# A graph layer with routed experts: five fields per edge record, node tiles spread over the sort, and a new order of loads, stores and statistics

## The reference

```python
xn = layernorm(x)
# 1: edges. segment_sum over src of edge_weight * xn[dst], beside xn itself
h   = concat([xn, segment_sum(edge_weight[:, None] * xn[dst], src, N)], axis=1)
gnn = relu(h @ gnn_W + gnn_b)
# 2: mixing of each node's channels: scaled projection to 768 channels, batch norm over the nodes,
#    relu, a grouped product, linear attention within groups of 32, projection back to 256
mix = expmap0(residual_projection(attention(batchnorm(project(logmap0(xn))))))
x   = x + gnn + mix
# 3: two of eight experts for each node
xt      = layernorm(x)
logits  = xt @ Wr + br                       # [3125, 8]
w, e    = top 2 of softmax(logits), w normalised to 1
y_e     = gelu((xt * ln_g[e] + ln_b[e]) @ W1[e] + b1[e]) @ W2[e] + b2[e]   # W1: 256 x 1024
out     = x + sum over both experts of w * y_e
```

## Time and profile before

| | |
|---|---|
| timed runs | 1204.49, 1205.29, 1206.28 us |
| profiled execution | 1207.6 us, span of its instructions 1205.8 us |
| TensorE (PE), busy | 990.7 us, 82% of the span |
| VectorE (DVE) | 770.8 us, 64% |
| POOL (GpSimd) | 636.9 us, 53% |
| ScalarE (ACT) | 590.9 us, 49% |
| mean granted TensorE clock | 0.899 of 2.4 GHz |
| DMA | 106.10 MB, mean 88 GB/s |

### The profile page before, as it was taken

How to read it: one execution, slowest core, us unless ns; L and a number is a source line. 1 busy time by engine, 2 the same in 40 slices (tenths; PEclk the granted TensorE clock), 3 DMA queues, 4 the chain that set the end, 5 groups by cost and what they waited for, 6 DMA issues and landing times.

```text
span 1205.8 us, 20167 instructions
## 1 busy us (share of the span) xinstructions
PE 990.7 (82%) x5432; PEld 800.6 (66%) x5433; DVE 770.8 (64%) x1705; ACT 590.9 (49%) x1528; POOL 636.9 (53%) x610
## 2 busy tenths in 40 slices
PE   2789859996687677777777767299999999999995
PEld 1356535553466566666565436299999999999995
DVE  9999956664577777777777788634444444444441
ACT  0455425556867776666765653133333333333331
POOL 4392247777777777776766750214443333333332
PEclk9799969997888888888888877599999999999998
DMA  7012123333333333333333449732222222222221
GB/s 171 24 41 89 33 58 103 104 105 104 102 101 101 104 101 102 105 97 92 97 97 96 133 161 377 264 93 37 35 38 39 39 35 35 35 39 36 40 36 18
DMA packets 55071, 106.10 MB, mean 88 GB/s; under 512 B 15337, under 2 KB 37070, under 8 KB 52822
## 3 DMA queue, kind: packets, MB, share of 16 engines
q0 software_dynamic: 31312, 70.38, 23.4%
q1 hardware_dynamic: 23075, 33.97, 8.8%
q10 hardware_dynamic: 611, 0.92, 0.3%
HBM read 86.55 MB, written 18.69 MB: 87 GB/s over the span
## 4 chain that ended last, share of the span: by engine, by line
PE 51%; DVE 26%; issue 12%; DMA 3%; DVEq 3%; ACT 2%; POOL 2%; ACTq 0%; POOLq 0%
PE ps L759 17%; PE ps L769 16%; PE ps L630 7%; DVE arena_c L1226 6%; PE ps L677 5%; DVE arena_a L1157 4%; PE ps L639 4%; DVE arena_a L1151 2%; DMA arena_c<-y_d,arena_e 2%; POOL arena_c L513 2%; DVEq L1214 1%; PE ps L749 1%; DVE arena_c L1276 1%; ACT arena_e L860 1%; DVEq L1212 1%
## 5 line engine op out<-in xcount | busy, mean ns | idle before, releaser
L513 POOL DMA_INDIRECT arena_c<-y_d,arena_e x415 | 407.8, 983 | 147.6 <-issue 87.7
L630 PE MATMUL ps<-arena_c,arena_e 128*125 128x256 f32 x830 | 255.3, 431 | 113.7 <-DVE arena_c L1226 87.0
L630 PEld LDWEIGHTS ps<-arena_c,arena_e 128*125 128x125 f32 x830 | 161.0, 212 | 191.5 <-issue 155.4
L1226 DVE TENSOR_TENSOR arena_c<-arena_c,ps 125x256 f32 x415 | 172.5, 416 | 100.3 <-PE ps L630 85.5
L539 POOL DMA_INDIRECT out<-node,bn x56 | 101.0, 1804 | 250.1 <-DVE node L1506 247.1
L860 ACT ACTIVATE arena_e<-arena_e 128x125 f32<-128x125 bf16 x415 | 190.6, 509 | 70.1 <-PE ps L630 57.0
L984 ACT ACTIVATE arena_d<-ps,small 128x128 f32<-128x128 f32 x448 | 121.6, 383 | 186.5 <-PE ps L759 151.5
L769 PE MATMUL ps<-arena_c,arena_d 128*128 x896 | 202.5, 379 | 0.0
L769 PEld LDWEIGHTS ps<-arena_c,arena_d 128*128 128x128 f32 x896 | 166.0, 190 | 20.3
L759 PEld LDWEIGHTS ps<-node,arena_d 128*128 128x128 f32 x896 | 107.2, 196 | 2.6 <-DVE node L1498 1.2
L759 PE MATMUL ps<-node,arena_d 128*128 128x128 f32 x896 | 107.4, 279 | 0.8 <-DVE node L1498 0.8
(11 more groups left out here) (318 smaller groups left out, 1370.3 us busy)
## 6 DMA issues: line engine op xcount, KB each, us to landing
arena_c<-in_W SPq DMA_DIRECT2D x8, 1024.0 KB, 9.3
arena_a<-in_W SPq DMA_DIRECT2D x8, 1024.0 KB, 12.7
arena_c<-y_d,arena_e POOLq DMA_INDIRECT x415, 2.8
x<-in_x SPq DMA_DIRECT2D x5, 560.0 KB
z_d<-x SPq DMA_DIRECT2D x5, 560.0 KB
out<-x SPq DMA_DIRECT2D x5, 560.0 KB
y_d<-arena_c SPq DMA_DIRECT2D x15, 125.0 KB
y_d<-arena_a SPq DMA_DIRECT2D x10, 125.0 KB
```

What stands on the lines that cost most here:

```text
L513: pool.indirect_dma_start(ring[:, b % GR, :], None, io["y_d"], bass.IndirectOffsetOnAxis(gix[:, b:b + 1], 0)).then_inc(gth[b % GR], 16)
L630: nc.tensor.matmul(pair(b), sel[b % SR], ring[:, b % GR, :], start=True, stop=True).then_inc(g_mm, 1)
L1226: V.tensor_tensor(part, part, pair(b), ALU.add).then_inc(g_acc, 1)
```

## The change

- An edge record has five fields. `dst` is stored as one 16-bit number, 0x3000 + dst, whose bits are read as bfloat16 through the placing matmul, and read back as an integer with one VectorE operation. One of the two bit operations, two casts and the buffer behind them go.
- `tiles_to(k)` spreads the 15 node tiles over chunks 1 to 18 instead of 0 to 14.
- SP loads `x` only when `src` has landed. POOL makes the two masks first, then splits the weights (as soon as they have landed), and only then the other index rows and the zero fill. ScalarE waits for that fill before its sixth turned copy instead of before its first tile.
- Every third sum `max(ACC, 0) + X` (tiles 2, 5, ..., 23) is made by POOL in two operations; SP, TensorE and VectorE wait for its semaphore `n_p` at those tiles.
- The logits' matmul has 48 columns instead of 96. ScalarE's two roots stand after tile 23 and after tile 24. VectorE computes `rz` and `zbias` behind the choice of experts.
- SP waits for the first two fetched blocks, then loads W2 of experts 5 and 6, then `b2s`, then stores `out`.

```diff
-NF = 6
+NF = 5
+CODE = 0x3000
-WIDE = 12
+WIDE = 6
+def tiles_to(k):
+    return AHEAD + min((NT - AHEAD) * k // (NK - 1), NT - AHEAD)
+def third(t):
+    return (t + 1) // 3
...
         def _(sp):
+            sp.wait_ge(ld_src, 16)
             x_t = io["x"].rearrange("(t p) c -> p t c", p=T)
...
-            sp.wait_ge(zeroed, 1 + 2 * (SPARE // BQ // EG))
+            sp.wait_ge(zeroed, 1 + SPARE // BQ // EG)
...
-                sp.wait_ge(n_x, t + 5)
+                sp.wait_ge(n_x, t + 5 - third(t + 4))
+                sp.wait_ge(n_p, third(t + 4))
...
-            sp.dma_start(b2s, io["b2"].partition_broadcast(128)).then_inc(b_in, 16)
+            sp.wait_ge(xs_in[0], 16)
+            sp.wait_ge(xs_in[1], 16)
             for e in (5, 6):
                 load_w2(e)
+            sp.dma_start(b2s, io["b2"].partition_broadcast(128)).then_inc(b_in, 16)
...
# POOL
-            P.memset(zero, 0.0).then_inc(zeroed, 1)
-            pool.wait_ge(zeroed, 1)
-            empty = zero.bitcast(BF16).rearrange("p (b g e f) -> p b (g e) f", g=EG, e=GE, f=NF)
-            for b in range(SPARE // BQ // EG):
-                P.iota(empty[:, b, :, 0], [[0, 128]], base=512 * b, ...).then_inc(zeroed, 1)
-                P.iota(empty[:, b, :, 1], [[1, 128]], base=0, ...).then_inc(zeroed, 1)
+            (the masks in_tile and in_chunk, moved here from behind iota_g)
+            pool.wait_ge(ld_edges, 32)
+            chain(P.tensor_copy(field[:, 2, :], w_e))
+            chain(P.tensor_tensor(w_e, w_e, field[:, 2, :], ALU.subtract))
+            chain(P.tensor_copy(field[:, 3, :], w_e))
+            P.tensor_tensor(field[:, 4, :], w_e, field[:, 3, :], ALU.subtract).then_inc(e_field, 1)
             (jcol, spare, iota_c, iota_g)
-            pool.wait_ge(e_bits, 2)
-            P.tensor_copy(field[:, 1, :], bits_a)
-            P.tensor_copy(field[:, 0, :], bits_b)
-            (the weights' splitting)
+            P.memset(zero, 0.0).then_inc(zeroed, 1)
+            pool.wait_ge(zeroed, 1)
+            for b in range(SPARE // BQ // EG):
+                P.iota(empty[:, b, :, 0], [[1, 128]], base=CODE + 512 * b, ...).then_inc(zeroed, 1)
...
+            pool.wait_ge(g_acc, EB)
+            pool.wait_ge(mixed, 1)
+            for t in range(2, NT, 3):
+                chain(P.tensor_scalar(ACC[:, t, :], ACC[:, t, :], 0.0, None, ALU.max))
+                P.tensor_tensor(X[0:T, t, :], ACC[:, t, :], X[0:T, t, :], ALU.add).then_inc(n_p, 1)
# TensorE and ScalarE, behind chunk k
-                if AHEAD + k < NT:
-                    tile(AHEAD + k)
+                for t in range(tiles_to(k), tiles_to(k + 1)):
+                    tile(t)
# TensorE
-                if f == 1:
+                if f == 0:
                     mm.then_inc(e_tr, 1)
-                pe.wait_ge(n_x, t + 1)
+                if t % 3 == 2:
+                    pe.wait_ge(n_p, third(t))
+                else:
+                    pe.wait_ge(n_x, t + 1 - third(t))
# ScalarE
-            act.wait_ge(filled, 16)
             def turn_out(t):
+                if t == 5:
+                    act.wait_ge(filled, 16)
-                if t == 18:
+                if t == NT - 2:
                     act.wait_ge(row_in, 6)
                     nc.scalar.activation(tmpb, tmpa, ACT.Sqrt).then_inc(row_out, 1)
-                if t == 20:
-                    act.wait_ge(row_in, 7)
-                    nc.scalar.activation(tmpb, tmpa, ACT.Sqrt).then_inc(row_out, 1)
+            act.wait_ge(row_in, 7)
+            nc.scalar.activation(tmpb, tmpa, ACT.Sqrt).then_inc(row_out, 1)
             act.wait_ge(row_in, 8)
# VectorE
-            V.tensor_scalar(bits_a, dst_i, 127, None, ALU.bitwise_and).then_inc(e_bits, 1)
-            V.tensor_scalar(bits_b, dst_i, -128, None, ALU.bitwise_and).then_inc(e_bits, 1)
+            V.tensor_scalar(field[:, 0, :].bitcast(I16), dst_i, float(CODE), None, ALU.add).then_inc(e_field, 1)
...
-            chain(V.tensor_copy(high4, psb[:, 0, :, :]))
-            V.tensor_tensor(gix4, high4, psb[:, 1, :, :], ALU.add).then_inc(gix_ready, 1)
+            V.tensor_scalar(gix4, codes[:, 0, :, :], -float(CODE), 0.0, ALU.add, ALU.max).then_inc(gix_ready, 1)
...
             for t in range(NT):
-                V.scalar_tensor_tensor(X[0:T, t, :], ACC[:, t, :], 0.0, X[0:T, t, :], ALU.max, ALU.add).then_inc(n_x, 1)
+                if t % 3 != 2:
+                    V.scalar_tensor_tensor(X[0:T, t, :], ACC[:, t, :], 0.0, X[0:T, t, :], ALU.max, ALU.add).then_inc(n_x, 1)
...
-            v.wait_ge(row_out, 9)
-            chain(V.reciprocal(rz, tmpb))
-            chain(V.tensor_tensor(rz, rz, rstd, ALU.mult))
-            chain(V.scalar_tensor_tensor(zbias, mean_, -1.0, rz, ALU.mult, ALU.mult))
             (logits, choice of the two experts)
             V.tensor_tensor(e21, m2, m1, ALU.subtract).then_inc(row_in, 1)
+            v.wait_ge(row_out, 9)
+            chain(V.reciprocal(rz, tmpb))
+            chain(V.tensor_tensor(rz, rz, rstd, ALU.mult))
+            chain(V.scalar_tensor_tensor(zbias, mean_, -1.0, rz, ALU.mult, ALU.mult))
```

48 lines of the change are left out of this document (23 added, 25 removed).

## The result

The changed kernel took 1194.25 us in the median of its four runs (1188.17, 1188.55, 1199.95, 1200.26), the kernel before 1204.89 (1203.79 to 1206.28): a ratio of 0.991, 95% interval 0.9882 to 0.9939. The median is of two kinds of execution with nothing between them, about 1188 and about 1200; the profile that came with it is of the long kind (1200.26 us, span 1198.5). The same kernel profiled again (experiment 1) fell on the short kind (1188.2 us, span 1186.4). Both are read here, since the difference between them is larger than most parts of the change. An execution is called short or long by its time alone; the stage in which they part was seen in one short profile and in three long ones (result, experiments 3 and 4).

The account below looks back on a forecast made before the run. VectorE was taken to pace head and sort, TensorE the untouched expert matmuls (a third of the span). Gains of 1.0 + 8.1 + 2.5 + 4.1 = 15.7 us off 1205.3 gave 1189.6 us, range 1181 to 1198.

Parts of the forecast that it names:

- Head, 1.0: Start to 58 us: earlier `src`, held `x` and POOL's reordered work together gain 1.0 us.
- B: Rival, head: POOL's moved work starves VectorE's L1026, head 3.3 us later, 1193.9 us in all; chance 0.18.
- between the two: Head: 1.0 us gain taken between 3.3 us later (POOL blocks VectorE) and 3.7 earlier (VectorE trains not interrupted).
- Sort, 8.1: Sort's twenty chunks: one field fewer saves VectorE 0.403 us a chunk, 8.1 us, with VectorE still the bound.
- C: Rival, sort: TensorE takes over, 15 chunks stay at 4.34 us, 6.0 us kept, 1195.6 us in all; chance 0.08.
- Sort's end, 2.5: 154 to 169 us: last chunk at full clock 1.4, fewer transposes 0.4, one VectorE operation 0.6, descriptors 0.1.
- Token stage: 722 to 781 us: late roots end the tile 18 stall; logits 5 to 6 us earlier, net gain 4.1 us.
- the fetch goes out 1.8 us earlier: Token stage: the gates' store queues behind full DMA engines, so the first fetch goes at 771.5, 1.8 us earlier, not 5.
- Halving `WIDE` therefore can't matter much either way.: Token stage: 48 logits columns for 96 matter little, as the fetch waits for the gates' store; no size given.
- The stall of block 4, 2.0: Experts: POOL's first scatter waits for the last `out` store, delaying block 4's fetch; 2.0 us lost, bounds 0 and 5.
- D: Rival: gates stored earlier, no stall, head gains 3.7; 22.9 us gained in all, 1182.4 us; chance 0.14.
- E: Rival, experts: held transfers run at 128 GB/s, stall 27.5 us, 1215.1 us in all, slower; chance 0.05.

Follow-up runs that it names:

- experiment 1: The changed kernel itself, run again unchanged: seven times from 1188.20 to 1199.95 us, ratio 0.995 to the kernel before.
- experiment 3: Changed kernel with W2 and `b2s` not held behind the first fetches: median 1200.52 us; with logits also 96 wide, 1189.30 to 1191.10 us.
- experiment 4: Changed kernel with all 25 sums on VectorE: 1187.96, 1191.18 and six from 1198.35 to 1200.57 us; with logits also 96 wide, median 1188.37 us.
- experiment 5: Kernel before with only the five-field record and POOL's new head order: 1280.38 to 1290.10 us, where the kernel before took 1296.9; ratio 0.9938.
- experiment 9: Changed kernel with logits 96 wide, two fifths of `out` stored early and `x` loaded beside the edges: 1185.93 to 1188.53 us, ratio 0.9853 to the kernel before.
- experiment 6: Kernel before with only the logits narrowed to 48 columns: median 1301.24 us, where the kernel before took 1296.9; ratio 1.0034.
- experiment 2: Changed kernel with logits 96 wide again: 1186.85 to 1192.31 us, ratio 0.9882 to the kernel before; run once more, ratio 0.9869.
- experiment 8: Changed kernel with logits 96 wide and two fifths of `out` stored right behind the gates: 1277.37 to 1280.86 us, ratio 0.9872 to the kernel before.
- experiment 7: Kernel before with only the two roots moved behind tiles 23 and 24, `rz` and `zbias` behind the routing: median 1294.27 us, ratio 0.9984.

## Why the prediction was right, and where it was not

The predicted 1189.6 lies 1.4 us from the short kind and 10 from the long; the median of four, 1194.25, falls between because two were of either. That it lies inside the stated 1181 to 1198 is luck: of eleven executions none took between 1188.6 and 1196.8 us, eight were long, and the median of the seven in experiment 1, 1199.12, lies outside. The sum held for the short kind, with terms too small in three places; the long kind it had no step for.

- **Head, 1.0.** Measured 1.7, and the source of it was not as told. `src` at 4.6 (said: about 4) and `x` never waited for: right. That a VectorE train once begun isn't interrupted: right for L1044 (4.41 us), which has begun when POOL's weights arrive, so B falls; wrong for L1048, whose train was stretched while POOL worked beside it. The price of POOL's moved work appeared in L1048 and L1052, some 1.9 and 1.0 us, which the sum had lumped into "between the two"; and holding `x`, taken as a gain, costs 0.5 to 1.1 us (experiments 5 and 9), since it brings the weights early enough for POOL to get in the way. All of the head's gain is POOL's new order with the shorter record (in experiment 5, without the hold, the sort starts 2.2 us earlier than before; with it 1.7). The two stretched rows agree with the Trainium skill (SBUF — State Buffer, Who interferes with whom), L1048 with its rule for two SBUF inputs beside a POOL operation that reads (L471 to L473), L1052 with its exclusive pair, taken first by the fill L479; by the same rule POOL's L470 was the one shut out by L1044, which the prediction had weighed only the other way round.
- **Sort, 8.1.** 7.4 and 7.6 measured over 19 steps, where 0.403 each is 7.7: right. VectorE's bound of 3.94: right. TensorE's 4.09 with a tile was 0.07 too high, since L611 gave the full sixth; the lag that it leaves is taken up without chunks free of a tile as well (experiment 5), so C falls, and the 2.2 us that the prediction gave to the spread are not there. The sort's gain is the record's alone (7.7 us over 19 steps in experiment 5).
- **Sort's end, 2.5.** With the chunk's own 0.4 that is 2.9; measured 3.7 and 3.8, of which 1.2 hang on the clock of the last chunk (1.4 had been said). In five of ten profiles a fall of the clock behind chunk 14 takes 1.4 to 1.8 back, which no step foresaw, and the 1.2 weren't lost in every execution before either (experiment 6).
- **Token stage.** The logits 5 to 6 us earlier: 5.1 in the short profile, 3.4 by the roots alone. The step mis-sized is "the fetch goes out 1.8 us earlier": it went 3.8 us earlier. Its mechanism is right: the gates' store was issued into the full engines, which were busy to about 752 us, and the fetch is released by `z_d<-gates`, 1.5 us behind the indices. The term that was too long is the store's landing, put at 771 or 48.5 us after the first sum, measured at 47.1. With the roots alone, and in all profiles with 96 columns, the fetch follows the indices and the gates take nothing of it. The fetch itself, 7.5 to 3.4, measured 3.0 and 3.5: right.
- **"Halving `WIDE` therefore can't matter much either way."** This is the step that failed in kind. It looked only at what the logits' end is worth behind the gates' store, and not at what half the columns do to TensorE's clock. In the profile of the long kind, which eight of eleven executions were by their times, the clock stayed at the 1.2 GHz level for the whole stage, the logits came 6.3 us later than before the change instead of 5 earlier (both by the long profile), and the time was 1197 to 1200. Experiments 2 and 6 show it from both sides.
- **The stall of block 4, 2.0.** 2.1 us in the short profile, but over three blocks and not as the single gap that was said; 4.2 in the long one, where the block after it takes 9.45, 1.5 of it because its L788 runs 5.15 us instead of 3.62 and the granted clock is 0.81 between 800 and 808 us. Cause as said: POOL's first scatter waits for the last store of `out` and goes 23.3 us behind the first normalising (18.7 before); experiments 3 and 8 take the stall of block 4 away. The size is partly luck: the last store was put at 24.5 us and came 1.1 earlier, by which the sum would give 0.9 for block 4; it shows 0.9 in the short profile, and the other 1.2 are in blocks 5 and 6, where the prediction had nothing left. D falls with the head and the stall, though 2.0 of the 2.5 us that it gave to earlier gates came; E falls.

Short kind against the sum: head 1.6, sort and its end 11.5, fetch and its start 8.2, stall 2.1: 1.6 + 11.5 + 8.2 - 2.1 = 19.2 us, where 15.7 were predicted. The difference is 0.6 in the head, 0.9 in the sort and its end, 2.0 in the fetch's start and 0.1 in its length, less 0.1 of stall. By the times, the short kind is only 16.7 us under the kernel before (1188.2 for 1204.9): the profile of before that both sums start from was a longer execution, 2.7 us over that median. So by the times the sum was only 1.0 us short, and part of what the table shows as gained is what that one execution had lost.

Open: why the stage settles at the upper level in three of eleven executions and not in the others. The short profile's clock is already up at the first sum, the three long ones' is at 0.50 there and stays. But entering high isn't enough: in experiment 6 it was up at the first sum and still fell. Open too is why the times of experiment 5 lie 10 us apart, and what decides behind which of the chunks without a tile the clock falls.

## What to carry to other kernels

When a matmul is made narrower, read the granted clock of its stage before and after: fewer columns can cost more than they save, and only in some executions, so take several and look at them one by one before trusting a median. Follow a load that is moved through everything that it now lets start early, since a helper engine that begins sooner can slow the engine that sets the pace. Held transfers need a place: name the idle stretch in the DMA windows, put what must land first into it, and look at what then waits. Before a difference of one or two microseconds between two profiles is put down to an edit, look for a group of matmuls that ran at the other clock in one of them.

## What the runs showed of the hardware

- TensorE's granted clock stayed at 0.50 for 35 us, in 20 of them with the engine busy 5.00 of every 5.00 us (float32 matmuls of 48 and 125 columns); with 96 columns on the same schedule it was at 1.00 again 5 us after the first sum in all six profiles, and either outcome came with 48.
- On one occasion, on a chip of its own, POOL's gathers paused, over long stretches after every eighth. Experiment 7's timeline:

```profile
241.27 0.94 POOL L513 DMA_INDIRECT arena_c<-y_d,arena_e  x1 [2.06 <-remote]
242.52 0.95 POOL L513 DMA_INDIRECT arena_c<-y_d,arena_e  x1 [0.30 <-issue]
...
250.04 0.94 POOL L513 DMA_INDIRECT arena_c<-y_d,arena_e  x1 [0.30 <-issue]
253.00 0.95 POOL L513 DMA_INDIRECT arena_c<-y_d,arena_e  x1 [2.02 <-remote]
```

  Each such gap is 2.0 us where the others are 0.30, released by something that the profile calls remote (17 times in this profile, 30.7 us) or, later on, put down to TensorE's L630. The other occasions have no such release. POOL's idle time before its 415 gathers is 234 us for 148, and from the first gather to the first sum it took 646 us instead of 554, which is the 90 us; the sort, the token stage and the experts kept their durations. Why is open.
- A POOL cast of 0.52 us took 3.24 beside a gapless train of VectorE scalings (L470 and L1044 of the changed kernel).
- The same 32 matmuls of the experts' first block took 5.17 to 6.79 us over the profiles, with a granted clock of 0.73 down to 0.54 over them, in kernels that don't differ there.
